# First convolution, last pair: 24 tent-sampled halves and 13 gathered tiles instead of 16 and 17

## The chip, the core and the metric

One core of one Trainium2 chip. Its engines run their own instruction streams in order and meet at semaphores: PE (matmuls and transposes), DVE and ACT (elementwise work), POOL (here it only issues gathers), SP (here it only issues DMAs). The metric is the device time of one execution in microseconds: 6645.84, the median of three runs (6641.96 to 6651.39). Lower is better.

## The reference

Eight images of 32 channels, 80 x 80, f32. Two residual layers. The first (L0) normalises, convolves to 18 offsets a pixel, samples nine taps at offset positions, and multiplies by a weight. The second applies that twice (here: first convolution C1, second convolution C2), with a mask on each tap. Cut to what matters for C1:

```python
om1 = conv2d(x, w_om1, b_om1)                  # 27 channels: 9 x (dy, dx), 9 masks
o1, o2, m1 = jnp.split(om1, 3, axis=1)
out = modulated_deform_conv(x, concat(o1, o2), sigmoid(m1), w_dcn1)
out = gelu(batchnorm(out, ...), approximate=False)

# modulated_deform_conv, for pixel (y, x) and tap k:
py = y - 1 + k // 3 + off[k, 0]
px = x - 1 + k % 3 + off[k, 1]
samp = bilinear_gather(x, py, px) * mask[k]    # four corners, zero outside the image
out = einsum('bckhw,ock->bohw', samp, weight)
```

A bilinear sample is also a sum over all rows and columns with the weights max(0, 1 - |p - q|), a tent in each direction, as long as the position lies in the rows that are summed.

## The kernel before, in words

The images are worked on in four pairs p = 0 to 3. For L0, C1 and C2 each pair has tiles of work. C1 samples a pair in two ways:

- **Gathered tiles** (16 x 16 pixels of both images; 25 cover a pair). POOL issues 36 indirect DMAs a tile (four units of nine taps, line 900) out of a table in HBM, into the four units of G. A unit of G is free again when DVE has summed it, so POOL is at most one tile ahead. DVE scales a unit (L2139) and adds its halves (L2153), PE turns and sums it (L1157), ACT copies it to SBUF (L1542), PE multiplies by the weights (L1244), ACT writes the GELU (L1559).
- **Halves** (two rows of 64 columns of both images, without gathers). For each tap PE multiplies a tent in x by a window of columns into two PSUM banks, one for each side of the row (`taps_half`, L1216; 4 matmuls with two passes each, shown as x8). DVE multiplies both by the tent in y (`weight_half`, L2250) into PRODS1, one buffer for each side, filled with three taps and then summed over 15 rows by PE (`reduce_half`, L1229, 15 transposes); so three groups of three taps, two sides. ACT copies each group (L1712), PE projects (L1253), ACT writes the GELU (L1555).

Two halves make a strip of four rows and share one preparation: the offset convolution on PE (L1091, with a column row L1097), ACT's copy of it (L1521), PE's turning (L1040), the mask on ACT (L1534), DVE's tent in y (L1898 to L1916). SP stores the x offsets to xo1 in HBM and loads them spread over the partitions into TX1 (five taps, then four); ACT makes tents of them in place (`tents1`, L1489 and L1491). TX1 is there once, so a load for the next half waits until PE has used these taps for the half before it.

The order is written out by hand: `schedule` walks through the same list for every engine, and `mix` turns a string into steps. "g" is a gathered tile alone (`consume`), "f" a tile and a half interleaved on all engines (`consume_both`), "d" and "x" have L0 tiles in them and don't occur in pair 3. In pair 3 the strings are gf, ff, ff, then fff three times, then ff: 17 tiles, 16 halves. Behind each of the first six strings PE, ACT and DVE build three pieces of a table of C2 (`build_step`, L968, L1456, L1815), and SP stores them. In f an odd half prepares the next strip (offset convolution late, after the ninth tap), and ACT waits for the tents of the next half between the third and the fourth unit of the tile.

`C1_ROWS` says which rows of a pair are done by halves: 32 to 63 in pair 3, 32 to 47 in the others, 64 of the 80 columns. Ahead of the first tile `columns1` turns the columns that the windows need into XT1 (L1003), in groups of eight rows. When the last step is over, DVE folds the ranges, SP brings back X, `calibrate` sets constants for C2, and C2 runs in rounds of a gathered tile and a strip.

Of the kernel before, what the change touches and what calls it, by code (L numbers as in the profile page):

```python
# [49 lines left out]
C1_ROWS = {0: (32, 48), 1: (32, 48), 2: (32, 48), 3: (32, 64)}  # L50
# [22 lines left out]
def build_program(nc, x, w_off, b_off, w_dcn, par, ident_d, base_y_d, base_x_d, bbase_d, out):  # L73
# [10 lines left out]
    with ctx:  # L84
# [68 lines left out]
        TX1F = {p: [lent(lender(p), lent_at(p) + 128 * k0, 128 * (k1 - k0)) for k0, k1 in TX_TAPS] for p in C1_ROWS}  # L153
        TX1 = {p: lent(lender(p), lent_at(p), 128 * TAPS).rearrange("p (k b n) -> p k b n", k=TAPS, b=2) for p in C1_ROWS}
        TY1 = {p: lent(lender(p), lent_at(p) + 1152, IDXS * WY1).rearrange("p (n w) -> p n w", w=WY1) for p in C1_ROWS}
# [60 lines left out]
        TAP = BTP + [OUT[1]]  # L216

# [139 lines left out]
        def column_groups(p):  # L357
            first, end = C1_ROWS[p]
            r0, r1 = first - 1 - BELOW1, end + 1 + WY1 - 1 - BELOW1
            return r0, [(r, min(8, r1 - r)) for r in range(r0, r1, 8)]  # L360
# [64 lines left out]
        def mix(on, c, kinds, gseg, at, dseg, at_d, cseg, at_c, then=""):  # L425
            before = ()
            for i, kind in enumerate(kinds):
                seg = dseg if kind == "d" else gseg
                done = sum(k != "d" for k in kinds[:i])
                done_d = sum(k in "dx" for k in kinds[:i])  # L430
                t = done_d + at_d if kind == "d" else done + at
                halves = at_c + kinds[:i + 1].count("f")
                ahead = (cseg, halves) if (kinds + then)[i + 1:i + 2] == "f" else None
                closes = i + 1 == len(kinds)
                prep = after_next(seg, t, c.n)
# [66 lines left out]
        def schedule(eng, on):  # L502
# [14 lines left out]
            for p in C1_ROWS:  # L517
# [155 lines left out]
        def _(sp):  # L673
# [93 lines left out]
            class on:  # L767
# [40 lines left out]
                def consume_both(step, half):  # L808
                    if half.prep:
# [127 lines left out]
        def _(pe):  # L937
            class on:
# [265 lines left out]
                def taps_half(half, k):  # L1204
# [5 lines left out]
                    if h or k:  # L1210
                        pe.wait_ge(weighted1, 18 * h + 2 * k)
                    row = strip_row(seg, t // 2) + t % 2 * 2 + k // 3 - 1 - BELOW1 - r0
                    for side in range(2):
                        ps_ = slice(XW * side, XW * side + XW)
                        for im in range(2):
                            last = nc.tensor.matmul(BTP[side][64 * im:64 * im + 64, 0:TAPW1], TX1[p][ps_, k, im, :],  # L1216
                                                    XT1[p][ps_, im, row:row + WY1, :].rearrange("p w c -> p (w c)"),
                                                    start=True, stop=True)
                        last.then_inc(taps1, 1)
# [28 lines left out]
                def project_half(half):  # L1248
                    pe.wait_ge(main.samp_ready, half.v + 8)
# [8 lines left out]
                def consume_both(step, half):  # L1258
# [35 lines left out]
                    on.project_half(half)  # L1294

# [141 lines left out]
        def _(act):  # L1437
            class on:
# [262 lines left out]

                def consume_both(step, half):
# [4 lines left out]
                    def half_sample(gr):  # L1707
                        act.wait_ge(prod_used, step.wg + 2 * (gr + 1) + GROUPS)
                        if gr == 0:
                            act.wait_ge(main.projected, step.v + 2)  # L1710
                        from_ = RED[1][0:TPG * C, 0:256].rearrange("p (h n) -> p h n", h=2)
                        last = nc.scalar.activation(SAMP1[half.seg.p][:, gr], from_, ACT.Copy)  # L1712
                        if gr < GROUPS - 1:
                            last.then_inc(group_sampled, 1)
                        else:
                            last.then_inc(main.samp_ready, 2)

# [3 lines left out]
                    half_sample(0)  # L1721
# [3 lines left out]
                    half_sample(1)  # L1725
# [6 lines left out]
                    half_sample(2)  # L1732
# [20 lines left out]
        def _(dve):  # L1753
# [15 lines left out]
            class on:  # L1769
# [104 lines left out]
                def columns1(p, built, halves):  # L1874
# [368 lines left out]
                def weight_half(half, k):  # L2243
                    gr, j, p = k // TPG, k % TPG, half.seg.p
                    for side in range(2):
                        at = 2 * gr + side
                        if j == 0:
# [4 lines left out]
                            in0=BTP[side][:, 0:TAPW1].rearrange("p (w c) -> p w c", w=WY1),  # L2252
                            in1=TY1[p][:, (half.t % 2 * 2 + side) * TAPS + k, :].unsqueeze(2).to_broadcast([128, WY1, C]),
                            op=ALU.mult).then_inc(weighted1, 1)

# [186 lines left out]
```

## Time and profile before

| | |
|---|---|
| median of 3 runs | 6645.84 us |
| the profiled execution | 6641.73 us |
| its span, first to last instruction | 6639.8 us |
| PE busy | 5752.4 us (87%) |
| PE weight loads busy | 4624.7 us (70%) |
| DVE busy | 4548.5 us (69%) |
| ACT busy | 2140.5 us (32%) |
| POOL busy | 4601.9 us (69%), 4752 gathers |
| mean granted PE clock | 0.93 |

The stage in question, the last pair of C1, is at about 3456 to 4241 us of the span. Busy shares over the whole span mix L0 (no gathers), C1 and C2; what bounds one stage is read from its own stretch. POOL's time between two gathers is not counted as busy. The clock of PE has two levels, 1.2 and 2.4 GHz; a granted clock of 0.88 in a stretch means that part of it ran at the lower one, where the same matmuls take about twice as long.

### The profile page before, as it was taken

What the parts mean: (1) busy time and instruction counts of PE and PEld (TensorE: products, weight loads), DVE (VectorE), ACT (ScalarE), POOL (GpSimd) and SP (SyncE); (2) the same over time, 40 slices, a digit from 0 to 9 for tenths busy, and PEclk for the clock granted to TensorE, in tenths of its full rate; (3) what the DMA queues carried; (4) which work ended last, traced back from release to release, by engine and by line L of the source; (5) the groups of instructions that cost most, each with busy time, mean ns of one, the idle gap of its engine ahead of it and who ended that gap; (6) DMA issues with size and microseconds to landing.
All of it is one profiled execution on the core that took longest, in us unless ns stands there. A gap on an engine that the chain in (4) does not pass through costs nothing. (4 is left out here: it accounts for less than half of the span.)

```text
span 6639.8 us, 129061 instructions
## 1 busy us (share of the span) xinstructions
PE 5752.4 (87%) x50305; PEld 4624.7 (70%) x50305; DVE 4548.5 (69%) x8684; ACT 2140.5 (32%) x3416; POOL 4601.9 (69%) x4765
## 2 busy tenths in 40 slices
PE   6997888987888988888977777799989989998996
PEld 6886776766777757777754555577767767776775
DVE  6886776866777857777854555577666766776775
ACT  1222222222222222222222222254434444443442
POOL 0005777777777777777777777777777777777776
PEclk9997999998999989999978888899989989998998
DMA  5333343435343433443332222333333333333333
GB/s 149 100 100 108 106 113 110 116 88 143 103 113 107 116 88 105 111 110 102 106 84 78 74 71 74 93 88 88 84 90 94 91 80 103 91 88 86 89 85 76
DMA packets 511330, 647.82 MB, mean 98 GB/s; under 512 B 118856, under 2 KB 414120, under 8 KB 502824
## 3 DMA queue, kind: packets, MB, share of 16 engines
q0 software_dynamic: 152064, 311.73, 18.6%
q1 hardware_dynamic: 358696, 328.04, 17.5%
q8 instruction: 412, 6.75, 0.4%
q14 instruction: 158, 1.29, 0.1%
HBM read 593.26 MB, written 46.15 MB: 96 GB/s over the span
## 5 line engine op out<-in xcount | busy, mean ns | idle before, releaser
L900 POOL DMA_INDIRECT G<-table,IDX x4752 | 4587.8, 965 | 1992.9 <-issue 1930.8
L2340 DVE TENSOR_TENSOR ARENA<-ARENA,OUT 128x864 f32<-128x864 f32 x936 | 937.9, 1048 | 130.6 <-PE RED L1142 97.8
L2139 DVE TENSOR_TENSOR G<-G,WPS 128x1152 f32<-128x1152 f32 x528 | 711.5, 1348 | 432.9 <-DMA G<-table,IDX 431.7
L1547 ACT ACTIVATE SAMP<-RED 96x384 f32<-96x384 f32 x688 | 335.4, 487 | 1907.2 <-PE RED L1365 815.8
L1142 PE MATMUL RED<-IDENT,ARENA 128*96 128x128 f32 x7344 | 880.6, 280 | 76.2 <-DVE ARENA L2340 76.2
L1142 PEld LDWEIGHTS RED<-IDENT,ARENA 128*96 128x96 f32 x7344 | 820.6, 129 | 121.1 <-issue 117.4
L1346 PE MATMUL BTP<-PAD,ARENA 80*128 x2304 | 744.9, 446 | 56.1 <-DVE ARENA L2132 29.5
L1091 PE MATMUL OFF<-PAD,ARENA 128*54 128x128 f32 (+1 forms) x10944 | 740.9, 293 | 19.5 <-ACT PAD L1447 6.8
L1091 PEld LDWEIGHTS OFF<-PAD,ARENA 128*54 128x54 f32 (+1 forms) x10944 | 659.9, 133 | 128.5 <-issue 98.9
L1216 PE MATMUL BTP<-X 64*64 64x480 f32 x2880 | 396.4, 621 | 199.5 <-DVE ARENA L2250 139.6
L1542 ACT ACTIVATE SAMP<-RED 96x384 f32<-96x384 f32 x448 | 218.3, 487 | 1068.6 <-PE RED L1157 547.9
L1346 PEld LDWEIGHTS BTP<-PAD,ARENA 80*128 80x128 f32 x2304 | 398.0, 193 | 185.7 <-issue 95.1
L1355 PE MATMUL RED<-IDENT,ARENA 128*96 128x128 f32 x3840 | 497.3, 277 | 0.0
L1355 PEld LDWEIGHTS RED<-IDENT,ARENA 128*96 128x96 f32 x3840 | 423.5, 127 | 83.1 <-DVE PAD L2132 22.4
L1172 PE MATMUL RED<-IDENT,ARENA 128*96 128x128 f32 x3888 | 458.0, 276 | 0.0
L1172 PEld LDWEIGHTS RED<-IDENT,ARENA 128*96 128x96 f32 x3888 | 424.8, 127 | 22.5 <-issue 22.0
L2250 DVE TENSOR_TENSOR ARENA<-BTP,X 128x480 f32<-128x480 f32 x504 | 317.8, 651 | 166.6 <-PE BTP L1216 115.7
L1346 PE MATMUL OUT<-PAD,ARENA 80*128 x1152 | 413.7, 441 | 0.0
L1229 PEld LDWEIGHTS RED<-IDENT,ARENA 128*96 128x96 f32 x2520 | 281.2, 130 | 120.5 <-issue 119.1
L1229 PE MATMUL RED<-IDENT,ARENA 128*96 128x128 f32 x2520 | 320.1, 282 | 47.3 <-DVE ARENA L2250 45.5
L2340 DVE TENSOR_TENSOR ARENA<-ARENA,WPS 128x864 f32<-128x864 f32 x312 | 314.0, 1047 | 56.2 <-PE RED L1142 56.2
L1521 ACT ACTIVATE OFFS<-OFF,BOFF 54x128 f32<-54x128 f32 (+1 forms) x512 | 185.3, 362 | 486.2 <-PE OFF L1091 402.6
(221 smaller groups left out, 7392.1 us busy)
## 6 DMA issues: line engine op xcount, KB each, us to landing
ARENA<-wtab SPq DMA_DIRECT2D x416, 400.0 KB
G<-table,IDX POOLq DMA_INDIRECT x4752
ARENA<-xo SPq DMA_DIRECT2D x96, 720.0 KB
table<-TB SPq DMA_DIRECT2D x64, 384.0 KB, 2.7
X<-xo SPq DMA_DIRECT2D x80, 160.0 KB
X<-xo SPq DMA_DIRECT2D x80, 128.0 KB
X<-x SPq DMA_DIRECT2D x3, 3200.0 KB, 19.0
out<-X SPq DMA_DIRECT2D x20, 320.0 KB
```

What stands on the lines that cost most here:

```text
L900: pool.indirect_dma_start(G[:, b, k, :], None, tables[seg.table], bass.IndirectOffsetOnAxis(ap=IDX[:, q, b * TAPS + k:b * TAPS + k + 1], a ...
L1091: last = nc.tensor.matmul(out_, WOFF[s][:, k, cols], in_, start=(k == 0), stop=(k == TAPS - 1 and not strip))
L1142: last = nc.tensor.matmul(RED[b % 2][0:TPG * C, gr * 128:(gr + 1) * 128], PROD[gr][:, sft, :], IDENT[:, :], start=(sft == 0), stop=(sft == ...
L1172: last = nc.tensor.matmul(RED[1][0:TPG * C, gr * 128:(gr + 1) * 128], PROD[gr][:, sft, :], IDENT[:, :], start=(sft == 0), stop=(sft == 8), ...
L1216: last = nc.tensor.matmul(BTP[side][64 * im:64 * im + 64, 0:TAPW1], TX1[p][ps_, k, im, :], XT1[p][ps_, im, row:row + WY1, :].rearrange("p ...
L1229: last = nc.tensor.matmul(out_, PRODS1[half.seg.p][side][:, w, :], IDENT[:, :], start=(w == 0), stop=(w == WY1 - 1), is_transpose=True)
L1346: nc.tensor.matmul(TAP[c % TAPB][:, 0:TAPW], TXB[tt][:, im, k, :], XT[:, bass.ds(bases[k] + (im * H + row) * C, TAPW)], start=True, stop=T ...
L1355: last = nc.tensor.matmul(RED[1][0:TPG * C, gr * 128:(gr + 1) * 128], PRODS[gr][:, w, :], IDENT[:, :], start=(w == 0), stop=(w == WY - 1), ...
L1547: nc.scalar.activation(SAMP[:, x], RED[x][0:TPG * C, 0:GROUPS * 128].rearrange("p (g n) -> p g n", g=GROUPS), ACT.Copy).then_inc(z.samp_re ...
L2139: nc.vector.tensor_tensor(out=slots, in0=slots, in1=WEIGHTS[q][:, b * TAPS:(b + 1) * TAPS, :].rearrange("p k s -> p (k s)").unsqueeze(2).t ...
L2250: nc.vector.tensor_tensor(out=PRODS1[p][side][:, :, j * C:(j + 1) * C], in0=BTP[side][:, 0:TAPW1].rearrange("p (w c) -> p w c", w=WY1), in ...
L2340: nc.vector.tensor_tensor(out=PROD[gr].rearrange("p (dy dx) (j c) -> p j dy dx c", dy=3, j=TPG), in0=win.rearrange("p j dy (dx c) -> p j d ...
```

## The change

In pair 3 the rows 32 to 79 are done by halves: 24 halves (12 strips) and 13 gathered tiles. Twelve halves, always the odd ones, are a new kind of step, "h": a half with no tile beside it (`consume_half`). Since no tile needs them there, RED[0] and OUT[1] serve as a second pair of tap banks (`TAPS_ALONE`), and a tap waits for the weighing of the tap two before it, not one (`behind`). The strings are gfh, fhfh five times, fh; the builds stand behind the first six of them, as before. XT1 grows by eight rows and a cleared margin, TX1 and TY1 of pair 3 move. The copy of a group out of RED[1] (`sample_half`) is taken out of `consume_both` unchanged. Cut to its core (`consume_half` stands in it three times: for PE, for ACT and for DVE):

```diff
-C1_ROWS = {0: (32, 48), 1: (32, 48), 2: (32, 48), 3: (32, 64)}
+C1_ROWS = {0: (32, 48), 1: (32, 48), 2: (32, 48), 3: (32, 80)}
...
+        TAPS_ALONE = BTP, [RED[0], OUT[1]]
...
-            r0, r1 = first - 1 - BELOW1, end + 1 + WY1 - 1 - BELOW1
+            r0, r1 = first - 1 - BELOW1, min(H + 1, end + 1 + WY1 - 1 - BELOW1)
...
+                if kind == "h":
+                    k = halves - 1
+                    prep = None
+                    if k % 2 and k + 1 < len(cseg.tiles):
+                        prep = (cseg, k // 2 + 1, 0, c.n, cseg.first // 2 + k // 2 + 1)
+                    half = Step(cseg, k, 0, c.u, c.v, c.u % 2, cseg.first + k, c.n, prep, before, closes, ahead, c.wg, False, c.built)
+                    on.consume_half(half)
...
-                    for k, kinds in enumerate(("gf", "ff", "ff")):
-                        mix(on, c, kinds, g, 2 * k, None, 0, s, max(0, 2 * k - 1), "f")
-                        builds_of(on, c, range(3 * k, 3 * k + 3), KB["t", PAIRS], GSEG[PAIRS], False)
-                    on.finished(ENDS[1])
-                    for k in range(3):
-                        mix(on, c, "fff", g, 6 + 3 * k, None, 0, s, 5 + 3 * k, "f")
-                        builds_of(on, c, range(3 * k, 3 * k + 3), KB["t", PAIRS + 1], GSEG[PAIRS + 1], False)
-                    mix(on, c, "ff", g, 15, None, 0, s, 14)
+                    for k, kinds in enumerate(("gfh", "fhfh", "fhfh", "fhfh", "fhfh", "fhfh", "fh")):
+                        if k == 3:
+                            on.finished(ENDS[1])
+                        mix(on, c, kinds, g, tiles, None, 0, s, halves, "f" if k < 6 else "")
+                        tiles, halves = tiles + sum(kind != "h" for kind in kinds), halves + sum(kind != "g" for kind in kinds)
+                        if k < 6:
+                            builds_of(on, c, range(3 * (k % 3), 3 * (k % 3) + 3), KB["t", PAIRS + k // 3], GSEG[PAIRS + k // 3], False)
...
-                        pe.wait_ge(weighted1, 18 * h + 2 * k)
+                        pe.wait_ge(weighted1, 18 * h + 2 * max(0, k + 1 - behind))
...
+                def consume_half(half):
+                    def alone(k):
+                        if k == 1:
+                            pe.wait_ge(main.samp_ready, half.v + 2)
+                        on.taps_half(half, k, TAPS_ALONE[k % 2], 2 if k else 1)
+
+                    for k in range(4):
+                        alone(k)
+                    on.reduce_half(half, 0, 0)
+                    alone(4)
+                    on.reduce_half(half, 1, 0)
+                    alone(5)
+                    if half.prep:
+                        on.convolve(*half.prep)
+                    on.reduce_half(half, 0, 1)
+                    alone(6)
+                    on.reduce_half(half, 1, 1)
+                    alone(7)
+                    alone(8)
+                    if half.prep:
+                        on.turn_offsets(*half.prep)
+                    pe.wait_ge(main.out_read, half.u + 2)
+                    on.reduce_half(half, 0, 2)
+                    on.reduce_half(half, 1, 2)
+                    on.project_half(half, 4)
...
+                def consume_half(half):
+                    on.sample_half(half, 0)
+                    if half.prep:
+                        on.offsets(*half.prep)
+                    on.sample_half(half, 1)
+                    if half.ahead:
+                        on.tents1(*half.ahead, 0)
+                    if half.prep:
+                        on.mask(*half.prep)
+                    on.sample_half(half, 2)
+                    on.finish(half, 4)
+                    if half.ahead:
+                        on.tents1(*half.ahead, 1)
...
+                    within = sum(count for _, count in groups)
+                    if within < lent_at(p) // R2:
+                        nc.vector.memset(XT1[p][:, :, within:, :], 0.0)
...
+                def consume_half(half):
+                    for k in range(TAPS):
+                        on.weight_half(half, k, TAPS_ALONE[k % 2])
+                        if k == 2:
+                            for tile_ in half.before:
+                                on.finish(*tile_)
+                    if half.prep:
+                        on.prepare(*half.prep)
+                    if half.closes:
+                        on.finish(half.seg, half.t, half.u, half.po)
```

SP in h does what it does for the half of an f: the stores of new offsets, then the two loads for the next half.

On PE, behind the first f of pair 3 (its last projection is the first row), the kernel before has a build and then the next f: a tap, the offset convolution of a tile, a tap, its turning, and the tile's first unit.

```order
L1253 MATMUL OUT<-ARENA,WDCN 32x128 x6
L968 MATMUL BTP<-IDENT,PAD 128x64 x36
L1216 MATMUL BTP<-X 64x480 x4
L1091 MATMUL OFF<-PAD,ARENA 54x128 x18
L1216 MATMUL BTP<-X 64x480 x4
L1044 MATMUL OFF<-IDENT,OFFS 128x118
```

At the same place the changed kernel has an h (its lines stand 17 lower: L1233 taps, L1246 reductions, L1108 convolution, L1270 projection). From the second tap to the third reduction:

```order
L1233 MATMUL RED<-X 64x480 x2
L1233 MATMUL OUT<-X 64x480 x2
L1233 MATMUL BTP<-X 64x480 x4
L1233 MATMUL RED<-X 64x480 x2
L1233 MATMUL OUT<-X 64x480 x2
L1246 MATMUL RED<-IDENT,ARENA 96x128 x15
L1233 MATMUL BTP<-X 64x480 x4
L1246 MATMUL RED<-IDENT,ARENA 96x128 x15
L1233 MATMUL RED<-X 64x480 x2
L1233 MATMUL OUT<-X 64x480 x2
L1108 MATMUL OFF<-PAD,ARENA 54x128 x18
L1114 MATMUL OFF<-X 54x128 x2
```

The taps alternate between BTP and the pair RED and OUT, and the convolution for the next strip stands behind the sixth tap; nothing of a tile lies between them. The build comes behind this step.

On ACT, an f with an odd half has this, from the copy of its new offsets to its end, in the kernel before: the tents of the next half, the last unit of the tile, the last group of the half, the mask, and both results.

```order
L1521 ACTIVATE OFFS<-OFF,BOFF 54x128 x2
L1489 ACTIVATE X<-X 128x640
L1491 ACTIVATE X<-X 128x640
L1542 ACTIVATE SAMP<-RED 96x384
L1712 ACTIVATE ARENA<-RED 96x256
L1534 ACTIVATE MASK<-OFF 128x36
L1559 ACT_TABLE_LOAD
L1559 ACTIVATE PAD<-OUT,SHF,SCL 64x2x16x8
L1555 ACTIVATE PAD<-OUT,SHF,SCL 64x2x64
```

In the changed kernel the same stretch of an h:

```order
L1569 ACTIVATE OFFS<-OFF,BOFF 54x128 x2
L1755 ACTIVATE ARENA<-RED 96x256
L1537 ACTIVATE X<-X 128x640
L1539 ACTIVATE X<-X 128x640
L1582 ACT_TABLE_LOAD
L1582 ACTIVATE MASK<-OFF 128x36
L1755 ACTIVATE ARENA<-RED 96x256
L1603 ACT_TABLE_LOAD
L1603 ACTIVATE PAD<-OUT,SHF,SCL 64x2x64
```

The offsets stand one group earlier, the tents still ahead of the last group, and the mask, now with a load of its table, ahead of it too.

## Rows read from the trace of the kernel before

**Rows 1.** Busy time in a stretch: us each, count, PE clock, DMA share, GB/s
```profile
3501.50:4240.80 739.30, 571.76 (x4698) 389.16 (x4696) 380.68 (x706) 181.92 (x324) 562.89 (x580) 0.88 0.28 74
```

**Rows 2.** Waits of 3501 to 4241: us in total, times, longest
```profile
POOL G L900 <- issue: 176.4, 579, 0.3
...
ACT X L1489 <- DMA X<-xo: 62.7, 7, 9.3
```

**Rows 3.** Timeline of PE: start, length, line, shapes, [idle before it]; stage's ends
```profile
3498.04 1.51 PE L1157 MATMUL RED<-IDENT,ARENA 128*96 128x128 f32 x6 [7.75 <-DVE ARENA L2153]
...
3551.02 1.83 PE L968 MATMUL BTP<-IDENT,PAD 64*128 64x64 f32 x12
...
4239.89 0.90 PE L1253 MATMUL OUT<-ARENA,WDCN 96*32 96x128 f32 x12
```

**Rows 4.** Timeline of POOL behind the stage
```profile
4286.51 0.94 POOL L900 DMA_INDIRECT G<-table,IDX  x1 [11.37 <-DVE SUM L2160]
```

**Rows 5.** Timeline of PE: one f step and the build behind it
```profile
3605.07 1.88 PE L1216 MATMUL BTP<-X 64*64 64x480 f32 x8
3607.49 3.10 PE L1091 MATMUL OFF<-PAD,ARENA 128*54 128x128 f32 x36 [0.55 <-DVE X L1916]
...
3635.16 1.81 PE L1229 MATMUL RED<-IDENT,ARENA 128*96 128x128 f32 x15 [1.36 <-DVE ARENA L2250]
...
3640.62 1.83 PE L968 MATMUL BTP<-IDENT,PAD 64*128 64x64 f32 x12
```

**Rows 6.** Timeline of PE: pieces of later f steps
```profile
3708.15 1.84 PE L1229 MATMUL RED<-IDENT,ARENA 128*96 128x128 f32 x15
3709.92 0.84 PE L1244 MATMUL OUT<-SAMP,WDCN 96*32 96x128 f32 x6
3710.74 1.03 PE L1216 MATMUL BTP<-X 64*64 64x480 f32 x8
3711.71 0.86 PE L1157 MATMUL RED<-IDENT,ARENA 128*96 128x128 f32 x6
...
3768.19 2.20 PE L1091 MATMUL OFF<-PAD,ARENA 128*54 128x128 f32 x36
...
3770.68 0.84 PE L1244 MATMUL OUT<-SAMP,WDCN 96*32 96x128 f32 x6
...
3873.70 0.44 PE L1040 MATMUL OFF<-IDENT,OFFS 118*64 118x54 f32 x8
3874.08 0.85 PE L1253 MATMUL OUT<-ARENA,WDCN 96*32 96x128 f32 x12
```

**Rows 7.** Timeline of DVE
```profile
3693.45 0.18 DVE L1898 SCALAR_TENSOR_TENSOR X<-OFF,X 128x18 f32<-128x18 f32 x1 [10.11 <-ACT MASK L1534]
...
3696.98 1.22 DVE L2250 TENSOR_TENSOR ARENA<-BTP,X 128x480 f32<-128x480 f32 x2
...
3711.81 1.22 DVE L2250 TENSOR_TENSOR ARENA<-BTP,X 128x480 f32<-128x480 f32 x2 [0.46 <-PE BTP L1216]
```

**Rows 8.** Timeline of ACT
```profile
3731.26 1.28 ACT L1559 ACT_TABLE_LOAD   x1
3732.56 0.59 ACT L1559 ACTIVATE PAD<-OUT,SHF,SCL 64x256 f32<-64x256 f32 x1
...
3735.00 0.49 ACT L1456 ACTIVATE TB<-BTP 128x384 f32<-128x384 f32 x1
...
3770.80 0.74 ACT L1521 ACTIVATE OFFS<-OFF,BOFF 54x128 f32<-54x128 f32 x2 [3.57 <-PE OFF L1097]
3780.68 0.83 ACT L1489 ACTIVATE X<-X 128x640 f32<-128x640 f32 x1 [9.14 <-DMA X<-xo]
...
3782.39 0.49 ACT L1542 ACTIVATE SAMP<-RED 96x384 f32<-96x384 f32 x1
3782.77 0.37 ACT L1712 ACTIVATE ARENA<-RED 96x256 f32<-96x256 f32 x1
```

**Rows 9.** Timeline of PE: the first tap behind that build
```profile
3739.89 1.88 PE L1216 MATMUL BTP<-X 64*64 64x480 f32 x8 [0.81 <-issue]
```

More of the change, by code:

```diff
@@ L428, in mix @@
                 seg = dseg if kind == "d" else gseg
-                done = sum(k != "d" for k in kinds[:i])
+                done = sum(k not in "dh" for k in kinds[:i])
                 done_d = sum(k in "dx" for k in kinds[:i])
                 t = done_d + at_d if kind == "d" else done + at
-                halves = at_c + kinds[:i + 1].count("f")
-                ahead = (cseg, halves) if (kinds + then)[i + 1:i + 2] == "f" else None
+                halves = at_c + sum(k in "fh" for k in kinds[:i + 1])
+                ahead = (cseg, halves) if (kinds + then)[i + 1:i + 2] in ("f", "h") else None
                 closes = i + 1 == len(kinds)
+                if kind == "h":
[5 more added lines that the diff above has]
+                    on.consume_half(half)
+                    before = ((cseg, k, c.u, c.u % 2),)
+                    c.n += prep is not None
+                    c.half, c.u, c.v, c.wg, c.drain = c.half + 1, c.u + 1, c.v + 2, c.wg + 6, True
+                    continue
                 prep = after_next(seg, t, c.n)
@@ L808, in consume_both @@
                 def consume_both(step, half):
+                    on.consume_half(half)
+                def consume_half(half):
                     if half.prep:
@@ L1202, in consume_pair, with taps_half @@
                     on.project_pair(step, dense, UNITS - 1)
-                def taps_half(half, k):
+                def taps_half(half, k, banks=BTP, behind=1):
                     seg, t, p, h = half.seg, half.t, half.seg.p, half.i
@@ L1215, in taps_half @@
                         for im in range(2):
-                            last = nc.tensor.matmul(BTP[side][64 * im:64 * im + 64, 0:TAPW1], TX1[p][ps_, k, im, :],
+                            last = nc.tensor.matmul(banks[side][64 * im:64 * im + 64, 0:TAPW1], TX1[p][ps_, k, im, :],
                                                     XT1[p][ps_, im, row:row + WY1, :].rearrange("p w c -> p (w c)"),
@@ L1246, in project_tile, with project_half @@
                     last.then_inc(main.projected, 1)
-                def project_half(half):
-                    pe.wait_ge(main.samp_ready, half.v + 8)
+                def project_half(half, sampled=8):
+                    pe.wait_ge(main.samp_ready, half.v + sampled)
                     for gr in range(GROUPS):
@@ L1294, in consume_both @@
                     on.project_half(half)
+                def consume_half(half):
+                    for e in tb_evac:
+                        pe.wait_ge(e, half.built)
+                    for side, e in enumerate(xt1_evac):
+                        pe.wait_ge(e, column_evacs(half.seg.p, side))
+                    def alone(k):
[21 more added lines that the diff above has]
+                    on.project_half(half, 4)
                 def dense_done(u):
@@ L1700, in consume_pair, with sample_half @@
                             on.tents1(*step.ahead, im)
+                def sample_half(half, gr):
+                    act.wait_ge(prod_used, half.wg + 2 * (gr + 1) + GROUPS)
+                    if gr == 0:
+                        act.wait_ge(main.projected, half.v + 2)
+                    from_ = RED[1][0:TPG * C, 0:256].rearrange("p (h n) -> p h n", h=2)
+                    last = nc.scalar.activation(SAMP1[half.seg.p][:, gr], from_, ACT.Copy)
+                    if gr < GROUPS - 1:
+                        last.then_inc(group_sampled, 1)
+                    else:
+                        last.then_inc(main.samp_ready, 2)
+                def consume_half(half):
[11 more added lines that the diff above has]
+                        on.tents1(*half.ahead, 1)
                 def consume_both(step, half):
@@ L1705, in tile_sample @@
                         on.sample(step.v + (1, 3, 4, 5)[b], 0)
[L1707 to L1716, printed above, removed]
                     if step.prep:
@@ L1720, in consume_both @@
                     tile_sample(0)
-                    half_sample(0)
+                    on.sample_half(half, 0)
                     tile_sample(1)
@@ L1724, in consume_both @@
                         on.mask(*step.prep)
-                    half_sample(1)
+                    on.sample_half(half, 1)
                     tile_sample(2)
@@ L1731, in consume_both @@
                     tile_sample(3)
-                    half_sample(2)
+                    on.sample_half(half, 2)
                     if half.prep:
@@ L2241, in consume, with weight_half @@
                         on.finish(seg, step.t, u, po)
-                def weight_half(half, k):
+                def weight_half(half, k, banks=BTP):
                     gr, j, p = k // TPG, k % TPG, half.seg.p
```

12 lines of the change are left out of this document (8 added, 4 removed).

## The prediction

> **What bounds the kernel now.** I read the stretches first, then the waits, then the timelines. In the sixteen steps of the last pair of the first convolution that take a gathered tile and a half together (I call such a step f), POOL is busy 562.89 us of 739.3 with 580 gathers [rows 1]; its 579 gaps sum to 176.4 us and are its own issue [rows 2]. 562.9 + 176.4 = 739.3: POOL waits for nobody here. A gather takes 739.3 / 580 = 1.275 us, a tile (36 gathers) 45.9 us, and the f steps run at (4239.89 + 0.85 - 3501.5) / 16 = 46.2 us each [rows 1, 3]. So POOL bounds this stage, while PE is busy 571.76 us of it. Behind the stage POOL stands still for 11.37 us, until the first sum of the second convolution frees a unit of G [rows 4]: the four units of the next tile are full by then. A stage that ends later moves everything behind it by the same amount, and one that ends earlier gives its gain on.
>
> **What the change takes from POOL.** Four tiles: 4 x 36 x 1.275 = 183.6 us. That is the most it can bring, and it counts only if the rest keeps up with 45.9 us for a tile. Now a pair of steps comes to each tile: an f, and a step with a half alone (h). What a pair takes on the other engines is the question; I lay it out in order of time.
>
> **The f step with no gather to wait for.** POOL has more than 45.9 us for a tile in every pair below, so all units lie ready. One f that follows a half with new offsets, as each f outside the builds now does, starts at 3605.07 and its successor's place comes at 3640.62: 35.55 us, in which PE waits 1.36 us for a weighing behind the last gather, against some 0.1 us where the units are there: 34.3 us [rows 5]. 
>
> **The h step, from its first tap (T = 0).** Pieces, start to start: a tap 0.97 (3710.74 to 3711.71), a reduction of 15 transposes 1.77 (3708.15 to 3709.92), the offset convolution with its extra row 2.49 (3768.19 to 3770.68), turning 0.38, projecting 0.85 [rows 6]. DVE's two weighings of a tap start 1.07 us after it (3710.74, 3711.81) and take 1.22 [rows 6, 7].
> - With four banks, tap 2 waits for the weighing of tap 0: 2.33 instead of 1.94. Tap 3 stands at 3.45, the first two reductions at 4.42 and 7.16 with tap 4 between them. PRODS1 still has one buffer a side, so the weighing of tap 3 waits for both reductions (8.95), and tap 5 for that weighing: 9.7. Convolution 10.67 to 13.16. The four banks help in the taps 1 to 4 alone.
> - From there PE goes on: two reductions, taps 6 to 8, turning, and the last two reductions, which wait for the last weighing, end at about 24.0.
> - Beside it: ACT takes up the offsets at 13.2. From that row to the tents of the next half it is 9.88 us (3770.80 to 3780.68), 9.14 of them waiting for the transfer out to xo and back; 7 such waits make 62.7 us, so this is the rule [rows 2, 8]. Tents 23.1 to 24.8 (1.71). ACT now has the tents ahead of the mask and both ahead of the last sample: table load 1.30 (3731.26 to 3732.56), mask 0.20, sample 0.37: 26.7 [rows 8]. Projection ends at 27.5. So the stall that f has in every second step is moved into h, and no gather covers it.
> - DVE's preparing follows the mask: 3693.45 to 3696.98, 3.5 us [rows 7]; it holds the convolution of the next f, and that is inside the 34.3.
>
> h is 27.5 us. Where builds follow (six of the first eleven), ACT still has a table load, the finish (0.43) and two tents (1.5) first: 29.9; from its first build copy to the next tap are 4.89 us (3735.00 to 3739.89) [rows 8, 9]: 34.8. The last h has no new offsets, so no convolution and no transfer: its last reduction ends at 22.4 (DVE's weighings fill some of the place of the convolution), and sample and projection make it 23.6.
>
> **Two rules weighed.** The waits above are 9.0 us each, through a store and a load. The Trainium skill (DMA: Bandwidth & Descriptors, Anatomy of one DMA) gives a fixed cost of about 2.0 us for a DMA on the software path; two in a row would be an estimated 4 us, the tents would be ready before PE's last reduction, and h would end with it at 25.3. By that the stage is 11 x 2.2 = 24 us shorter. The rows have more than twice that, and I go by them. The other way: the skill (ScalarE: Activation LUTs, What ACT_TABLE_LOAD costs) counts a 1.38 us drain on top of each switch of tables, an estimated 11 x 1.38 = 15 us more for the mask's switch in h. Here the activation starts 1.30 us after the load started [rows 8], so I add nothing.
>
> **The rest of the edits.** The eighth column group and DVE's memset before the first tile: at the far end of that step PE waits 7.75 us for a gathered unit [rows 3], so nothing to see; without that cover one group more of seven, below 3 us. Taking the moved tents and tap banks: nothing in itself. POOL's queue only loses 144 gathers. SP gets four more sets of stores to xo and eight loads; in its queue, in h, the next half's loads stand behind these stores, which is the 9.88. What is queued behind ACT's wait for the transfer: mask, last sample, finish; behind those PE's projection and DVE's preparing, all counted.
>
> **The sum.** The first f ends at 3551.02 as before (gathers bound it). Then 6 x 34.8 + 5 x 27.5 + 23.6 + 11 x 34.3 = 208.8 + 137.5 + 23.6 + 377.3 = 747.2, so the stage ends at 4298.2 instead of 4240.7 [rows 3]: 57.5 us later. Where POOL was the bound with 45.9, a pair now takes 61.8 (69.1 with builds), and POOL has about 183.6 + 57.5 = 241 us of waiting. The profiled execution took 6641.73 us: 6699. The median is 6645.84, 4.1 above it: forecast 6703.
>
> **Bounds of the two unsure terms.** h: below, PE never waits in it (9 x 0.97 + 6 x 1.77 + 2.49 + 0.38 + 0.85 = 23.1); above, PE falls to the lower level behind the convolution, where taps take 1.88 for 1.03: the rest of h about doubles, 35. f: below 32.5, if it starts at the higher level (0.85 less for the tap, 0.9 for the convolution); above 36, as long as gathers make it. My 27.5 and 34.3 are sums of rows of the same instructions in the same order.
>
> **Rivals.**
> 1. *The transfer is shorter with fewer gathers about, or is hidden*: h 25.3, 24 us less: 6679. For it: POOL rests a quarter of the time. Against: seven waits of nearly one length, whatever POOL did.
> 2. *PE falls to the lower level within h*: its pauses (0.4, 0.8, 2.7) are new. 11 x 7.5 = 83 us more: 6786. Against: an f has pauses of 0.5 to 1.1 and runs at 1.03 a tap behind them; only the 2.7 is like those that cost the level.
> 3. *Faster: h runs at PE's issue rate.* The tents land before T = 18, no weighing holds a tap, f starts at the higher level: h 23.1 (30.4 with builds), f 32.5: 182.4 + 115.5 + 20.2 + 357.5 = 675.6, 14 us earlier than before: 6632. It turns at about 690 us, an h of 24.3 with an f of 32.5. For it: that is PE's work. Against: 9.88 us behind a convolution that can't start before 10.7 ends past 20.5, and the single PRODS1.
> 4. *No change*: half of both gains at once. (That the gathers don't go away can't be: the list of gathered tiles has 13.)
>
> **Chances.** Forecast 0.60 (6680 to 6728), rival 1 0.17, rival 2 0.12, rival 3 0.06, rival 4 0.05. About 0.2% (13 us) is what can be told from no change here. Slower 0.89, same 0.05, faster 0.06. For 8 in 10 I take the forecast, rival 1 with a margin below, and the near part of rival 2: 6656 to 6750.
>
> **What would show it.** POOL waiting for DVE's sums some 240 us in this stage; PE starting an f 61 to 63 us after the last where no builds lie; ACT idle 5 us or so before the first tents of every h (it samples in between) and PE idle 2 to 3 us before h's projection. An h of 23 to 24 us would prove me wrong, or POOL with no wait.

## The result, and the profile after

The changed kernel takes 6699.15 us, the median of three runs (6697.25 to 6707.76), against 6645.84: ratio 1.0083, interval 1.0066 to 1.01, so 53 us slower. 6703 was forecast. The profiled execution is the one of 6699.15 us, with a span of 6697.3.

The stretch of the stage first, as [rows 1] had it (busy time of PE, PE's weight loads, DVE, ACT, POOL, each with its count; PE clock, DMA share, GB/s), and two short ones that are read further below:

```profile
3501.50:4296.00 794.50, 671.66 (x5928) 444.89 (x5920) 434.82 (x802) 227.35 (x383) 436.77 (x462) 0.95 0.24 65
...
3618.90:3646.30 27.40, 22.84 (x224) 14.61 (x222) 11.92 (x24) 8.47 (x15) 14.96 (x16) 1.00 0.26 64
3646.30:3650.00 3.70, 3.07 (x24) 1.49 (x24) 3.49 (x7) 2.38 (x4) 0.00 (x0) 0.54 0.00 0
```

POOL's 562.89 us in 739.3 have become 436.77 in 794.5, and PE has 100 us more to do: twelve halves and the preparing for them came in. The waits of the same stretch answer to [rows 2] (us in total, times, longest):

```profile
POOL G L917 <- DVE SUM L2218: 220.2, 22, 25.3
...
POOL G L917 <- issue: 134.1, 440, 0.3
```

The first row is new. Before, POOL waited for nobody but itself; now it stands still for 220 us because no unit of G is free. The first convolution's last pair is therefore no longer set by the gathers. Its ends on PE answer to [rows 3]: the end of the first f, the first h behind it (its build is the fourth row, and the next f the last but one), and the last projection of the stage.

```profile
3549.51 0.90 PE L1270 MATMUL OUT<-ARENA,WDCN 96*32 96x128 f32 x12
3550.34 1.04 PE L1233 MATMUL BTP<-X 64*64 64x480 f32 x8
...
3577.44 0.85 PE L1270 MATMUL OUT<-ARENA,WDCN 96*32 96x128 f32 x12 [2.74 <-ACT ARENA L1755]
3578.22 1.88 PE L985 MATMUL BTP<-IDENT,PAD 64*128 64x64 f32 x12
...
3585.58 1.88 PE L1233 MATMUL BTP<-X 64*64 64x480 f32 x8 [0.70 <-issue]
...
4296.16 0.85 PE L1270 MATMUL OUT<-ARENA,WDCN 96*32 96x128 f32 x12 [0.53 <-ACT ARENA L1755]
```

The first f's own projection in the kernel before is the row

```profile
3550.19 0.90 PE L1253 MATMUL OUT<-ARENA,WDCN 96*32 96x128 f32 x12
```

From the last projection of the first f to that of the stage, start to start, are 4239.89 - 3550.19 = 689.7 us before [rows 3] and 4296.16 - 3549.51 = 746.6 now. I use this distance for every kernel below and call it the stage's length. It is 56.9 us longer, and the time of the program 53 to 58: all of the loss is here.

One h without builds, on PE, against the pieces of [rows 6], and the start of the f behind it:

```profile
3618.90 1.03 PE L1233 MATMUL BTP<-X 64*64 64x480 f32 x8
...
3628.84 0.62 PE L1233 MATMUL RED<-X 64*64 64x480 f32 x2 [0.84 <-DVE ARENA L2315]
...
3629.80 2.20 PE L1108 MATMUL OFF<-PAD,ARENA 128*54 128x128 f32 x36
...
3639.80 3.45 PE L1246 MATMUL RED<-IDENT,ARENA 128*96 128x128 f32 x30 [0.77 <-DVE ARENA L2315]
3645.53 0.85 PE L1270 MATMUL OUT<-ARENA,WDCN 96*32 96x128 f32 x12 [2.28 <-ACT ARENA L1755]
3646.31 1.80 PE L1233 MATMUL BTP<-X 64*64 64x480 f32 x8
3648.74 2.77 PE L1108 MATMUL OFF<-PAD,ARENA 128*54 128x128 f32 x36 [0.63 <-DVE X L1981]
...
3777.79 1.04 PE L1233 MATMUL BTP<-X 64*64 64x480 f32 x8
3780.22 2.26 PE L1108 MATMUL OFF<-PAD,ARENA 128*54 128x128 f32 x36 [1.40 <-DVE X L1981]
```

The convolution comes behind the sixth tap, 10.9 us into the step. The last reduction is over at 3643.25, but the projection waits 2.28 us for ACT. And this f begins at the lower clock level: its tap takes 1.80 us, not 1.03, and the granted clock of its first 3.7 us is 0.54, while the h had 1.00 (the two short stretches above). That is not the rule. Of the five f behind an h without builds, three begin at the higher level, as the one in the last two rows does (1.00 in its first 3.7 us), and then wait 1.40 us for DVE's preparing (L1981), which stands behind the late mask; these three take 33.5 us, the other two 34.0 and 35.8. What ACT does in the same step, as in [rows 8]:

```profile
3632.40 0.74 ACT L1569 ACTIVATE OFFS<-OFF,BOFF 54x128 f32<-54x128 f32 x2 [3.99 <-PE OFF L1114]
3636.91 0.38 ACT L1755 ACTIVATE ARENA<-RED 96x256 f32<-96x256 f32 x1 [3.76 <-PE RED L1246]
3642.01 0.83 ACT L1537 ACTIVATE X<-X 128x640 f32<-128x640 f32 x1 [4.73 <-DMA X<-xo]
...
3643.72 1.28 ACT L1582 ACT_TABLE_LOAD   x1
3645.01 0.20 ACT L1582 ACTIVATE MASK<-OFF 128x36 f32<-128x36 f32 x1
3645.11 0.37 ACT L1755 ACTIVATE ARENA<-RED 96x256 f32<-96x256 f32 x1
```

Offsets, then 9.61 us until the loads have come back from xo1, then tents, table load, mask, and only then the sample for which PE's projection waits.

Behind the stage POOL stands still for 48.94 us where it stood 11.37 [rows 4], so it cannot catch up with anything:

```profile
4341.39 0.94 POOL L917 DMA_INDIRECT G<-table,IDX  x1 [48.94 <-DVE SUM L2225]
```

### The profile page after: what moved, and what is told of

Read it like the earlier page. It is cut to its first block and busy times, and to the rows that moved or that the text cites. A ratio compares the mean times of both kernels' runs of the same rounds, so it can differ in the third digit from the quotient of the medians.

```text
span 6697.3 us, 131732 instructions
## 1 busy us (share of the span) xinstructions
PE 5856.4 (87%) x51581; PEld 4687.7 (70%) x51581; DVE 4607.1 (69%) x8781; ACT 2184.1 (33%) x3475; POOL 4450.0 (66%) x4621
## 5 line engine op out<-in xcount | busy, mean ns | idle before, releaser
L917 POOL DMA_INDIRECT G<-table,IDX x4608 | 4435.9, 963 | 2200.4 <-issue 1881.9
L1159 PE MATMUL RED<-IDENT,ARENA 128*96 128x128 f32 x7344 | 882.6, 280 | 76.4 <-DVE ARENA L2416 76.4
L2204 DVE TENSOR_TENSOR G<-G,WPS 128x1152 f32<-128x1152 f32 x512 | 689.9, 1348 | 321.0 <-DMA G<-table,IDX 319.6
L1159 PEld LDWEIGHTS RED<-IDENT,ARENA 128*96 128x96 f32 x7344 | 822.7, 130 | 121.0 <-issue 117.6
L1108 PE MATMUL OFF<-PAD,ARENA 128*54 128x128 f32 (+1 forms) x10944 | 736.0, 292 | 20.9 <-ACT PAD L1495 6.8
L1108 PEld LDWEIGHTS OFF<-PAD,ARENA 128*54 128x54 f32 (+1 forms) x10944 | 655.3, 132 | 125.0 <-issue 96.1
L1233 PE MATMUL BTP<-X 64*64 64x480 f32 x3072 | 412.9, 608 | 177.6 <-DVE ARENA L2315 117.9
L2315 DVE TENSOR_TENSOR ARENA<-BTP,X 128x480 f32<-128x480 f32 x552 | 348.2, 651 | 239.2 <-PE BTP L1233 175.3
L1403 PE MATMUL RED<-IDENT,ARENA 128*96 128x128 f32 x3840 | 498.8, 278 | 0.0
L1403 PEld LDWEIGHTS RED<-IDENT,ARENA 128*96 128x96 f32 x3840 | 424.5, 128 | 83.2 <-DVE PAD L2197 22.6
L1189 PE MATMUL RED<-IDENT,ARENA 128*96 128x128 f32 x3888 | 455.4, 275 | 0.0
L1189 PEld LDWEIGHTS RED<-IDENT,ARENA 128*96 128x96 f32 x3888 | 422.4, 127 | 22.1 <-issue 21.8
L1246 PEld LDWEIGHTS RED<-IDENT,ARENA 128*96 128x96 f32 x3240 | 349.2, 127 | 114.8 <-issue 105.4
L1246 PE MATMUL RED<-IDENT,ARENA 128*96 128x128 f32 x3240 | 395.5, 276 | 19.5 <-DVE ARENA L2315 17.0
```

What stands on the lines that cost most here:

```text
L917: pool.indirect_dma_start(G[:, b, k, :], None, tables[seg.table], bass.IndirectOffsetOnAxis(ap=IDX[:, q, b * TAPS + k:b * TAPS + k + 1], a ...
L1108: last = nc.tensor.matmul(out_, WOFF[s][:, k, cols], in_, start=(k == 0), stop=(k == TAPS - 1 and not strip))
L1159: last = nc.tensor.matmul(RED[b % 2][0:TPG * C, gr * 128:(gr + 1) * 128], PROD[gr][:, sft, :], IDENT[:, :], start=(sft == 0), stop=(sft == ...
L1189: last = nc.tensor.matmul(RED[1][0:TPG * C, gr * 128:(gr + 1) * 128], PROD[gr][:, sft, :], IDENT[:, :], start=(sft == 0), stop=(sft == 8), ...
L1233: last = nc.tensor.matmul(banks[side][64 * im:64 * im + 64, 0:TAPW1], TX1[p][ps_, k, im, :], XT1[p][ps_, im, row:row + WY1, :].rearrange(" ...
L1246: last = nc.tensor.matmul(out_, PRODS1[half.seg.p][side][:, w, :], IDENT[:, :], start=(w == 0), stop=(w == WY1 - 1), is_transpose=True)
```

## The experiments

Theory: POOL bound the stage before; the change frees it, but f and h together take longer than a tile's 45.9 us of gathers, because in h the offsets are made late and their way through HBM, the mask and the samples lie open at its end. Rivals: gathers still bound the stage after the change (or did not before); h is long because of its taps and reductions and not because of the offsets' way.

### 1 and 2: more gathers in both kernels

Each tile of the stage gets six gathers more, whose data nothing reads; the edit is the same in the kernel before (`p_before`) and the changed one (`p_after`).

```diff
+EXTRA = 6
...
+                    if b == 0 and seg is GSEG[PAIRS - 1]:
+                        for k in range(EXTRA):
+                            pool.indirect_dma_start(
+                                arena(6240 + 128 * k, 128), None, tables[seg.table],
+                                bass.IndirectOffsetOnAxis(ap=IDX[:, q, k:k + 1], axis=0),
+                            ).then_inc(z.gathered[b], 16)
```

> The kernel before, with six more gathers for each tile of the last pair of the first convolution (unit 0; they go to a place that nothing reads). POOL as the bound of that stage: 17 tiles x 6 x 1.275 us = 130 us longer, 6776 us. If PE or the transfers of the offsets set the pace there, POOL's time has some 10 us a tile to spare and the time stays within 30 us of 6646.

> The changed kernel with the same six gathers more for each of its 13 tiles. My theory (from the first f on, the pair of f and h on PE, DVE and ACT sets the pace with some 61 to 69 us, POOL needs 53.5 with the extra gathers): only the two tiles ahead of it pay, 2 x 7.65 = 15 us, so 6714 us, and POOL's wait for sums falls from 220 to some 140 us. If POOL still sets the pace: 13 x 7.65 = 99 us more, 6798 us.

The kernel before: 6786.5 us, 1.0201 (1.0184 to 1.0218) of the 6656.91 that the kernel before took beside it, so 130 us more. 17 x 6 x 1.275 = 130. POOL's waits there, from 3501.5 to 4360, are its own issue and nothing else:

```profile
POOL G L901 <- issue: 175.2, 575, 0.3
POOL ARENA L907 <- issue: 29.3, 96, 0.3
```

The changed kernel: 6725.28 us, 1.0111 (1.0094 to 1.0128). It was 1.0083 without the gathers, so they cost some 19 us where 13 x 6 x 1.275 = 99 us of POOL came in. POOL's waits, 3501.5 to 4300:

```profile
POOL G L918 <- issue: 137.2, 450, 0.3
POOL G L918 <- DVE SUM L2228: 132.0, 12, 17.1
POOL ARENA L924 <- issue: 18.9, 62, 0.3
```

The new gathers went into POOL's waiting, which fell from 220 to 132. The stage's length is unchanged, 746.4 us (3569.85 to 4316.22); what remains of the cost is in the first f, which waits for gathers in both kernels and ends 20 us later here (3 of them arose ahead of this pair). POOL bound the stage before, and does not now.

### 3: two banks for the taps of h

DVE weighs the taps from the same two banks. On PE:

```diff
-                        on.taps_half(half, k, TAPS_ALONE[k % 2], 2 if k else 1)
+                        on.taps_half(half, k)
...
-                    for k in range(4):
+                    for k in range(3):
                         alone(k)
                     on.reduce_half(half, 0, 0)
-                    alone(4)
+                    alone(3)
                     on.reduce_half(half, 1, 0)
+                    alone(4)
                     alone(5)
```

> The changed kernel without its second pair of tap banks: h takes its taps in the two banks and in the order that an f has (third group of reductions and the convolution stay where they are). Worked out from the same pieces: each tap then waits for the weighing before it, the convolution ends at 17.2 us of h instead of 13.2, and h is 31.6 instead of 27.4 us; 12 x 4.2 = 50 us longer, 6749 us. If h is set by something that banks don't touch (POOL, the clock), the time stays at 6699.

6792.81 us, 1.0209 (1.0192 to 1.0226): 84 us over the changed kernel, where the waits alone should have cost 50. PE in one h, and the third tap and the first reduction of another (the last two rows):

```profile
3632.15 1.03 PE L1233 MATMUL BTP<-X 64*64 64x480 f32 x8
3634.66 1.03 PE L1233 MATMUL BTP<-X 64*64 64x480 f32 x8 [1.47 <-DVE ARENA L2316]
3637.00 1.76 PE L1233 MATMUL BTP<-X 64*64 64x480 f32 x8 [1.30 <-DVE ARENA L2316]
3639.58 3.40 PE L1246 MATMUL RED<-IDENT,ARENA 128*96 128x128 f32 x15 [0.82 <-DVE ARENA L2316]
...
3662.80 4.27 PE L1246 MATMUL RED<-IDENT,ARENA 128*96 128x128 f32 x30 [0.21 <-DVE ARENA L2316]
3667.59 0.85 PE L1270 MATMUL OUT<-ARENA,WDCN 96*32 96x128 f32 x12 [0.53 <-ACT ARENA L1756]
...
3851.12 1.03 PE L1233 MATMUL BTP<-X 64*64 64x480 f32 x8 [1.30 <-DVE ARENA L2316]
3852.99 1.81 PE L1246 MATMUL RED<-IDENT,ARENA 128*96 128x128 f32 x15 [0.84 <-DVE ARENA L2316]
```

The waits for weighings are there (1.47, 1.30, 0.82), and behind the second of them the clock falls: a tap takes 1.76 us, the next reduction 3.40 instead of 1.8. The granted clock in a stretch from there (same columns as the stretch above):

```profile
3637.00:3643.50 6.50, 5.68 (x27) 3.38 (x31) 1.22 (x2) 0.00 (x0) 4.94 (x6) 0.51 0.20 50
```

0.51 is the lower level, 1.2 GHz. This h takes 36.2 us. The h of the last two rows has the same pauses and keeps a granted clock of 1.00 throughout; so does one more of the twelve. These two lie 32.3 us apart from projection to projection, the other ten 34.8 to 36.3. What was missed in the expectation is the mechanism of the prediction's second rival: the pauses cost their own length, some 4.8 us an h (32.3 against 27.5), and in ten of twelve h also the clock, some 3 to 4 us more. So the four banks, which seemed to help in four taps only, also kept the higher level in h: with them it stood at 1.00 in all. Why two of the twelve kept it here with the same pauses, these runs do not show.

### 4: the offset convolution early in h

PE convolves behind the second tap instead of the sixth, and turns the offsets behind the sixth; ACT samples the first group behind the offsets, and the second between mask and third.

```diff
-                    for k in range(4):
-                        alone(k)
+                    alone(0)
+                    alone(1)
+                    if half.prep:
+                        on.convolve(*half.prep)
+                    alone(2)
+                    alone(3)
...
-                        on.convolve(*half.prep)
+                        on.turn_offsets(*half.prep)
```

> The changed kernel with the offset convolution of h behind its second tap instead of its sixth, and on ACT the new offsets ahead of the first sample, the tents of the next half behind it, the mask ahead of the second sample. Theory: the transfer of the offsets (9.6 us from ACT's copy to the tents) and the mask's table load behind it end h; started 8.7 us earlier they lie under PE's work: h 25.5 instead of 27.4 us, 32.8 instead of 35.2 where builds follow, and the next f no longer waits for DVE's preparing (32.3 instead of 34.0): 6 x 2.4 + 5 x 1.9 + 5 x 1.7 = 32 us shorter, 6667 us. Rival: PE's own order ends h (its last reduction comes at 24.0 either way) and the transfer is hidden up to the last 0.5 us: within 8 us of 6699.

6682.09 us, 1.0039 (1.0024 to 1.0053): 29 us less than the changed kernel by the ratios. ACT in one h that begins at 3624.98:

```profile
3629.36 0.74 ACT L1571 ACTIVATE OFFS<-OFF,BOFF 54x128 f32<-54x128 f32 x2 [1.52 <-PE OFF L1114]
...
3639.13 0.83 ACT L1539 ACTIVATE X<-X 128x640 f32<-128x640 f32 x1 [3.05 <-DMA X<-xo]
...
3649.41 0.38 ACT L1757 ACTIVATE ARENA<-RED 96x256 f32<-96x256 f32 x1 [6.06 <-PE RED L1246]
```

The offsets' way is as long as before (9.77 us), but now ACT waits 6 us for PE at the end, and not PE for ACT. And PE:

```profile
3636.51 0.62 PE L1233 MATMUL RED<-X 64*64 64x480 f32 x2 [0.84 <-DVE ARENA L2317]
...
3645.86 3.45 PE L1246 MATMUL RED<-IDENT,ARENA 128*96 128x128 f32 x30 [1.15 <-DVE ARENA L2317]
3649.84 0.85 PE L1270 MATMUL OUT<-ARENA,WDCN 96*32 96x128 f32 x12 [0.53 <-ACT ARENA L1757]
3650.62 1.03 PE L1233 MATMUL BTP<-X 64*64 64x480 f32 x8
3651.59 2.27 PE L1108 MATMUL OFF<-PAD,ARENA 128*54 128x128 f32 x36
```

The 2.28 us before the projection are 0.53, and h takes 25.6 us instead of 27.4. The f behind it no longer waits for DVE's preparing (the last row, against 1.40 us at 3780.22 above), since the mask comes 8.5 us before h's end (3642.13), and it takes 32.0 us instead of 33.5 or more. All five f of this kind start at the higher level (1.03); in three of them that was so before, and what they gained is that wait. The stage is 715.7 us long: 31 of the 57 lost are back. 11 x 1.85 = 20 of them are h's own, 10 are in these five f. So the open end of h was more than half of the loss, and a third of its price was paid in the step behind it, which waited for what follows the mask, and in two of five also ran at the lower level.

### 5: the changed kernel once more

> The changed kernel once more, so that the two kernels beside it stand against it on one chip. Every theory: 0.8% above the kernel before (1.0066 to 1.01), steps with a half alone (h) of 27.4 us without builds and 35.2 with them, steps f of 33.3 to 34.0.

6704.63 us against 6646.09, 1.0087 (1.0072 to 1.0102); stage 3555.61 to 4301.80, 746.2 us. Four of its five f behind an h without builds start at the higher level and take 33.5 us, one takes 35.9. It stands for the two below, which ran beside it.

### 6: both reductions of a group together

On top of experiment 4, tap 4 no longer stands between the first two reductions, nor tap 6 between the next two:

```diff
                     on.reduce_half(half, 0, 0)
-                    alone(4)
                     on.reduce_half(half, 1, 0)
+                    alone(4)
                     alone(5)
                     if half.prep:
                         on.turn_offsets(*half.prep)
-                    on.reduce_half(half, 0, 1)
                     alone(6)
+                    on.reduce_half(half, 0, 1)
                     on.reduce_half(half, 1, 1)
```

> The kernel with the early convolution, and in each h both reductions of a group of taps directly behind each other, so that the one PRODS1 buffer of a side is free sooner (before, tap 4 lay between the first two and the last two reductions apart). Theory 1, with the transfer out of the way the single PRODS1 buffer is what holds PE in h: an h of 24.3 us instead of 25.6, 12 x 1.3 = 15 us less than the early convolution alone, ratio to before about 1.002. Theory 2, what is left of h is the chain of sampling and projecting on ACT at its end: h stays at 25.6, ratio 1.004. Theory 3, the closer reductions make longer pauses between taps and PE falls to its lower clock level, as with two banks: h 30 or more, ratio above 1.01.

6650.72 us, 1.0007 (0.9998 to 1.0015): no difference from the kernel before that can be told. h takes 24.0 us (24.3 expected), the stage 696.2 (3562.10 to 4258.31), 19.5 less than in experiment 4; 12 x 1.65 = 20. PE in the h from 3629.13:

```profile
3635.26 3.45 PE L1246 MATMUL RED<-IDENT,ARENA 128*96 128x128 f32 x30
...
3648.36 3.45 PE L1246 MATMUL RED<-IDENT,ARENA 128*96 128x128 f32 x30 [1.15 <-DVE ARENA L2317]
```

The single PRODS1 of each side held the weighings, and with them PE, as long as one of a group's two reductions stood behind a tap: the wait of 0.84 us before the sixth tap of experiment 4 (3636.51) is gone, and only the 1.15 before the last reductions is left. The granted clock of h stayed at 1.00.

### 7: the builds within h

On top of experiment 6, the 18 builds that stood in threes between the strings go into the twelve h, two and one in turn: one behind the last tap and one behind the last reduction, on RED[0] and OUT[1], which h no longer needs there.

```diff
+                    c.todo = [(KB["t", PAIRS + b // ITS], b % ITS, GSEG[PAIRS + b // ITS]) for b in range(2 * ITS)]
...
-                        if k < 6:
-                            builds_of(on, c, range(3 * (k % 3), 3 * (k % 3) + 3), KB["t", PAIRS + k // 3], GSEG[PAIRS + k // 3], False)
...
+                    for build in half.prep_builds[0:1]:
+                        pe.wait_ge(weighted1, 18 * half.i + 16)
+                        on.build_step(*build, False, banks=TAPS_ALONE[1])
...
+                    for build in half.prep_builds[1:2]:
+                        on.build_step(*build, False, banks=TAPS_ALONE[1])
```

> As the one before, and the 18 table builds of this stretch, which stood in threes between the steps of the first six halves, go one or two into each of the twelve h, behind its last taps and its last reduction, with a tap bank that is free there. Theory 1, a group of three builds costs 7.4 us between the steps because PE, ACT and DVE take turns there with nothing beside them: inside h a build costs 1.2 to 1.3 us, h is 25.5 us with one and 26.8 with two, the stage ends 20 to 25 us earlier than that of the kernel before, ratio 0.996 to 0.997. Theory 2, the builds' copies on ACT and DVE delay the tents, the samples and the weighings by as much as they took between the steps: no gain over the kernel without this edit, ratio about 1.002. Theory 3, the moved builds bring POOL back as the bound (45.9 us for a tile): not before f + h falls below 45.9, so not here; POOL still waits 100 us or more.

6615.98 us, 0.9957 (0.9945 to 0.9969): 30 us faster than the kernel before, and about 1.3% faster than the changed one. PE in an h with one build:

```profile
3638.31 1.00 PE L1237 MATMUL BTP<-X 64*64 64x480 f32 x8
3639.80 1.02 PE L989 MATMUL RED<-IDENT,PAD 64*128 64x64 f32 x6 [0.49 <-DVE ARENA L2330]
3640.66 0.97 PE L989 MATMUL OUT<-IDENT,PAD 64*128 64x64 f32 x6
3641.56 3.48 PE L1250 MATMUL RED<-IDENT,ARENA 128*96 128x128 f32 x30
3645.57 0.85 PE L1274 MATMUL OUT<-ARENA,WDCN 96*32 96x128 f32 x12 [0.53 <-ACT ARENA L1766]
3646.35 1.03 PE L1237 MATMUL BTP<-X 64*64 64x480 f32 x8
```

The build takes 1.76 us of PE at the higher level and fills the place where PE waited 1.15 us for the last weighing, so h is 25.1 us long with one (24.0 without). Between the strings three builds took about 9.6 us with their aftermath (a pair of projections lay 41.6 us apart with builds, 32.0 without). The stretch of the stage shows what bounds it now:

```profile
3563.00:4224.00 661.00, 615.72 (x5669) 417.05 (x5669) 412.99 (x762) 217.95 (x367) 403.60 (x424) 0.99 0.27 74
```

PE is busy 93% at a clock of 0.99; every f starts at the higher level now, also where builds lay ahead of it. The stage's length is 662.1 us (3562.07 to 4224.20), 27.6 less than before. (The profiled execution took 6637.74 us, 22 more than the median of the six. Against the profile of the kernel before, 11 us lie ahead of this pair and 12 behind the stage, where nothing was changed; why, the runs do not show.) POOL still waits, 178 us in the stage and behind it. An f of 32.0 and an h of 26.1 (the mean of eleven; two of them took 28.0) are 58.1 us for a tile of 45.9 us of gathers. By these numbers both engines would be nearer to each other with halves in place of two or three tiles and not four; but the halves replace a whole row of four tiles, and a split of a row was not tried.

## Why the prediction was right, point by point

| step of the prediction | predicted | measured |
|---|---|---|
| what bounded the stage before | POOL, at 1.275 us a gather | 102 gathers more cost 130 us (1.27 each) |
| f, no builds ahead | 34.3 us | 33.5 in three of five, 34.0 and 35.8 |
| f behind builds | 34.3 | 34.3, the mean of six (33.3 to 34.8) |
| h, no builds behind | 27.5 | 27.5, the mean of five (27.4 to 27.7) |
| h with builds | 34.8 | 34.8, the mean of six (34.6 to 35.2) |
| last h | 23.6 | 24.1 |
| end of the stage | 4298.2 | 4297.0 |
| profiled execution | 6699 | 6699.15 |
| POOL's waiting | 241 | 220 in the stage, 3.4 more at its end |

Within h the steps came out so, in us from its first tap (predicted, then measured): end of the convolution 13.16, 13.4; tents begin 23.1, 23.1; last reduction ends 24.0, 24.35; last sample ends 26.7, 26.6. The offsets took 9.61 us to become tents, where a row of before gave 9.88. Each of these terms was one interval between rows of the same instructions, not a sum of costs that the trace doesn't show.

What was mis-sized: POOL's waiting. I took 183.6 + 57.5 for granted. But of 144 gathers taken away, only 118 are missing in the stretch (580 to 462), since POOL goes on with 26 of the next tile, which cost 33 us here; and the gathers with their gaps took (436.77 + 134.1) / 462 = 1.236 us each, not 1.275, which gave 18 back (7 because the gaps of 22 gathers are counted with the wait before them, 11 because a gather was busy 0.945 us and not 0.970). 241 - 33 + 18 leaves 226, and 223.6 were seen.

In f the number held and its make-up in part did not, which is luck. The f behind builds begin at the lower level, as [rows 5] had it. But three of the five others begin at the higher level, against what was predicted; what they save by it, about 1.7 us in the first tap and the convolution, goes half into a longer wait for DVE's preparing, 1.40 us where [rows 5] has 0.55. The prediction called that wait "inside the 34.3" and put an f that starts at the higher level at 32.5: with the mask as late as it is, it is 33.5, and experiment 4, which takes the wait away, has 32.0.

The rivals.

*A shorter transfer*: it did not shorten, 9.61 us (9.5 to 10.1 over the stage) with a quarter of POOL's time idle. SP's own rows show a part that POOL doesn't touch: it issues the four stores from 3633.17 to 3636.37, and the two loads for which the first tents wait from 3637.61 to 3638.75, which is 4.3 us of the 9.61. In the kernel before, where POOL never rested, the four stores take 3.27 us to issue (from 3771.56) against 3.20. So of the two rules weighed, the estimate of 4 us worked out from the fixed cost of a DMA in the Trainium skill (DMA: Bandwidth & Descriptors, Anatomy of one DMA) does not fit the way of the offsets here, store and load and what lies between them; the trace has over twice that. What the estimate left out is above all the issue one by one: without its 4.3 us and ACT's copy (0.74) 4.5 us are left, 1.24 between the last store's issue and the first load's, and 3.26 from the second load's to the tents. And the drain which the Trainium skill (ScalarE: Activation LUTs, What ACT_TABLE_LOAD costs) counts beside a table load was rightly left out: the mask starts 1.29 us after the load's start (3643.72 to 3645.01).

*The lower level within h*: not in the changed kernel, whose h has a granted clock of 1.00; experiment 3 shows that it was near, since two banks brought it in ten of twelve h.

*Faster, with h at PE's issue rate*: it failed for the two reasons that were given against it, and experiments 4 and 6 removed one each. The turning point of 690 us was right as a length: in experiment 6 the stage was 696 long, and the time that of the kernel before. But the steps that were named for it, an h of 24.3 and an f of 32.5, do not lead to it: by the prediction's terms the 24.0 and 32.0 of experiment 6, shorter still, would make 681. The 15 us between are the builds, which cost 9.6 us a group there and not 7.3 (the f behind them starts at the lower level), and a last h of 22.5 instead of 21.1.

*No change*: not so, the interval begins at 1.0066.

## What to carry to other kernels

A busy engine that bounds a stage is relieved only down to what the others take for the same unit of work; work that out per step, with the waits, before moving work to them. Here the added step was 3.4 us longer than it had to be, all of it by the order inside (offsets that travel through HBM made late, two reductions of one buffer apart), and with the builds taken into it the same split is faster than the kernel before. What a step prepares late is paid again in the step behind it: here a late mask cost up to 1.4 us of waiting at the start of the next f.

## What the runs showed of the hardware that was not expected

- Pauses of PE of the same length did not always have the same clock behind them. In experiment 3 all twelve h have pauses of 1.47 and 1.30 us between single taps: ten fell to the lower level for a time (0.51 granted over 6.5 us of one), two stayed at 1.00. With pauses of 0.57 and 0.84 in the changed kernel's h it was 1.00 in all twelve.
- Behind an h without builds the changed kernel has a pause of 2.28, 2.43, 2.25, 2.37 or 2.55 us and a projection of 0.85; the granted clock of the first 3.7 us of the f that follows is 0.54, 1.00, 1.00, 1.00 and 0.60 in that order.
- Storing the offsets and loading them back took 9.5 to 10.1 us in the changed kernel. In the step shown, 4.3 of 9.61 us are SP's issue: 3.20 for four stores and 1.14 for two loads.
- A gather kept POOL busy 0.970 us in the stage before and 0.945 in the changed kernel's (562.89 / 580 and 436.77 / 462); the gap to the next is 0.305 us in both where POOL does not wait (176.4 / 579 and 134.1 / 440).
